# A two-bank maximum on VectorE: one reduction for two heads' score blocks in an attention layer

## What is computed

```python
x = x + attention(layernorm(x)) @ Wo + bo       # causal, scores / sqrt(256), softmax over the keys
x = x + quantised(layernorm(x)) @ quantised(W).T + bias   # blocks of 32, FP6 grid, scale = max|block| / 7.5
```

## Time and profile before

| | |
|---|---|
| median of three runs | 2117.28 us (2115.57 to 2119.65) |
| the profiled execution | 2120.14 us, span 2118.4 us |
| busy: PE, DVE, ACT, POOL | 95%, 82%, 64%, 37% of the span |
| mean granted TensorE clock | 0.985 of full speed |
| whole-unit reductions, L1108 | 1536 of 683 ns, 968.3 us |
| unit products, L1365 | 2560, 816.6 us |

### The profile page before, as it was taken

How to read it: one execution, slowest core, us unless ns; L and a number is a source line. 1 busy time by engine, 2 the same in 40 slices (tenths; PEclk the granted TensorE clock), 3 DMA queues, 4 the chain that set the end, 5 groups by cost and what they waited for, 6 DMA issues and landing times.

```text
span 2118.4 us, 36179 instructions
## 1 busy us (share of the span) xinstructions
PE 2012.2 (95%) x12037; PEld 792.0 (37%) x12037; DVE 1739.8 (82%) x4442; ACT 1365.3 (64%) x2905; POOL 783.3 (37%) x1099
## 2 busy tenths in 40 slices
PE   6799899999999999999999999999999999999994
PEld 3333333333333444343333344434333343333433
DVE  4797897878988787888888788796898998888875
ACT  5357666766766666667665666676666666777661
POOL 3323324231435454543324556363143443111232
PEclk9899999999999999999999999999999999999997
DMA  4441221313040322312122231221403112030000
GB/s 153 128 103 54 59 74 37 94 46 97 19 101 26 97 64 72 101 42 87 49 62 58 79 87 63 66 87 49 118 4 101 42 44 57 25 92 24 9 31 20
DMA packets 178327, 138.72 MB, mean 65 GB/s; under 512 B 54486, under 2 KB 178140, under 8 KB 178140
## 3 DMA queue, kind: packets, MB, share of 16 engines
q1 hardware_dynamic: 178140, 136.40, 23.3%
HBM read 85.20 MB, written 50.33 MB: 64 GB/s over the span
## 4 chain that ended last, share of the span: by engine, by line
PE 72%; DVE 16%; ACT 3%; issue 3%; SPq 2%; POOL 2%; DMA 2%; POOLq 0%; DVEq 0%; ACTq 0%
PE psum L1397 21%; PE psum L1380 19%; PE psum L1365 16%; PE psum L1463 7%; DVE max_parts L1108 7%; PE psum L1456 5%; DVE psum L1103 3%; ACT probs L911 2%; PE psum L1432 1%; SPq L633 1%; PE psum L1415 1%; ACT acc_sb L918 1%; PE psum L1485 1%; DMA out_shop<-ctx_scratch 1%; DVE max_parts L1103 1%
## 5 line engine op out<-in xcount | busy, mean ns | idle before, releaser
L911 ACT ACTIVATE probs<-psum 128x512 f32<-128x512 f32 (+3 forms) x2560 | 1213.3, 537 | 527.4 <-PE psum L1380 521.8
L1108 DVE TENSOR_REDUCE max_parts<-psum 128x1 f32<-128x512 f32 x1536 | 968.3, 683 | 130.0 <-PE psum L1365 125.6
L1380 PE MATMUL psum<-q_rows,k_rows 99*128 99x512 bf16 (+3 forms) x2560 | 857.4, 351 | 3.4 <-ACT probs L911 1.6
L1365 PE MATMUL psum<-k_rows,q_rows 96*128 96x512 bf16 (+3 forms) x2560 | 816.6, 350 | 25.8 <-DVE max_parts L1108 10.2
L1397 PE MATMUL psum<-probs,v_in 128*17 128x512 f32 (+3 forms) x5120 | 595.4, 537 | 10.6 <-ACT acc_sb L918 9.9
L1103 DVE CUSTOM_DVE_ANT_0 psum<-psum,causal 128x128 f32<-128x128 f32 (+3 forms) x1024 | 475.9, 519 | 133.4 <-PE psum L1365 130.2
L1380 PEld LDWEIGHTS psum<-q_rows,k_rows 99*128 99x128 bf16 x2560 | 237.2, 97 | 632.0 <-ACT probs L911 496.3
L748 POOL TENSOR_SCALAR_AFFINE_SELECT probs<-probs 128x512 f32<-128x512 f32 x256 | 165.2, 645 | 788.7 <-ACT probs L911 788.3
L1365 PEld LDWEIGHTS psum<-k_rows,q_rows 96*128 96x128 bf16 x2560 | 245.1, 98 | 277.8 <-DVE max_parts L1108 65.3
L1397 PEld LDWEIGHTS psum<-probs,v_in 128*17 128x17 f32 x5120 | 85.8, 95 | 226.9 <-issue 165.0
L1103 DVE DVE_READ_ACCUMULATOR2_ANT max_parts<- 128x1 f32 x1024 | 145.0, 142 | 0.0
(11 more groups left out here) (158 smaller groups left out, 1374.7 us busy)
## 6 DMA issues: line engine op xcount, KB each, us to landing
q_rows<-qk_scratch SPq DMA_DIRECT2D x384, 64.0 KB, 2.6
k_rows<-qk_scratch SPq DMA_DIRECT2D x384, 64.0 KB, 2.7
qk_scratch<-shop SPq DMA_DIRECT2D x56, 384.0 KB, 2.9
shop<-in_L_attn_x SPq DMA_DIRECT2D x19, 512.0 KB, 4.0
v_scratch<-shop SPq DMA_DIRECT2D x16, 544.0 KB, 4.0
v_in<-v_scratch SPq DMA_DIRECT2D x64, 136.0 KB, 2.6
ctx_scratch<-ctx_out SPq DMA_DIRECT2D x60, 128.0 KB, 1.7
out_shop<-in_L_attn_x SPq DMA_DIRECT2D x12, 512.0 KB, 5.4
```

Source lines behind the costliest of these rows:

```text
L911: nc.scalar.activation(probs[s % NPROBS][:, h, a:CHUNK], bank[SCORE_BANKS[n % 3]][:, a:CHUNK], ACT.Exp, scale=SCALE).then_inc(probs_ready, 1)
L1108: nc.vector.tensor_reduce(max_parts[k % 2][:, first:first + heads, t % TILES, c], ring_bank(UNIT_USE[n])[:, 0:heads * width] .rearrange("p ...
L1365: ins = nc.tensor.matmul(dst[:, i * width:(i + 1) * width], q_rows[u][0:ROWS, qc, first + i, t % TILES * P:(t % TILES + 1) * P], k_rows[u] ...
L1380: nc.tensor.matmul(bank[SCORE_BANKS[n % 3]][:, a:CHUNK], k_rows[u][0:ROWS + LEVELS, h, kb * P:(kb + 1) * P], q_rows[u][0:ROWS + LEVELS, qc ...
```

## The change

Where two neighbouring heads' whole units of one tile and one block of keys stand in the same slot and in neighbouring banks of which the first is 4 or 6 (an even use), VectorE reads both banks with one instruction that has two outputs, and counts `unit_used` up by two. It does so when the second unit's turn comes; the first unit's turn passes without an instruction. All other units are taken as before. PE's program is the same.

```diff
+UNIT_SLOT = {n: p for p in SLOTS for n in UNITS_AT.get(p, [])}
+
+
+def begins_pair(n):
+
+    if n + 1 >= len(UNITS):
+        return False
+    k, t, c, first, heads = UNITS[n]
+    return (c < QCS[k] and UNITS[n + 1] == (k, t, c, first + 1, 1) and UNIT_SLOT[n] == UNIT_SLOT[n + 1]
+            and UNIT_USE[n + 1] == UNIT_USE[n] + 1 and UNIT_USE[n] % 2 == 0)
...
+            def take_pair(n):
+                k, t, c, first, heads = UNITS[n]
+                dve.wait_ge(unit_ready, n + 2)
+                at_bank = RING_BANKS[UNIT_USE[n] % RING]
+                nc.vector.tensor_reduce(max_parts[k % 2][:, first:first + 2, t % TILES, c],
+                                        psum[:, at_bank:at_bank + 2, :], AX.X, ALU.max).then_inc(unit_used, 2)
...
                 for i in range(4):
                     for n in share(units, i, 4):
-                        take_unit(n)
+                        if n > 0 and begins_pair(n - 1):
+                            take_pair(n - 1)
+                        elif not begins_pair(n):
+                            take_unit(n)
```

## The result

The changed kernel takes 2205.45 us (median of four runs, 2204.66 to 2205.95), the kernel before 2116.81 us beside it. The ratio is 1.0405, with a 95% interval of 1.0392 to 1.0419: 86 us slower by the ratio, 89 by the two medians. The forecast was slower by 47 us, 2164; the stated range ended at 2203, and the ratio put on the 2117.28 us of the kernel before is 2203.0, so the result lies at the range's upper end. The sign was right and so was the main place, the size was little over half of what came.

The account below looks back on a forecast made before the run. The prediction took PE, busy 95%, to set the pace mostly, tightly coupled with DVE through four banks. Stalls of 59 us, less 7 hidden and 6 gained, made it 46 to 47 us slower: 2164 us, range 2128 to 2203.

Parts of the forecast that it names:

- The middle pairs' stall: Pairs of heads 1 and 2, values between: bank back after 3.21 us, wanted at 2.83; PE waits 0.38 us every full slot.
- The outer pairs: Pairs of heads 0 and 1 or 2 and 3: 0.70 us to spare in a full slot; 13 short pairs add 4.7 us.
- the 228 pairs before which DVE was behind: Remaining pairs, nothing held back for the second unit: first bank 0.53 us later; taken as zero, upper bound 43 us.
- the rival that gave 2186: DVE's backlog counts: half of the 43 us is added; chance 0.12, shared with two banks costing two instructions.
- The gain of 6 us: DVE's whole-unit reductions on the chain: 87 pairs there save 0.07 us each, 6 us.
- The 7 us taken off: Stalls hidden where values wait for ACT's accumulator copy anyway, or by few other gaps close behind: 7 us less loss.
- DVE's late start: DVE comes 0.52 us later out of a middle pair it waited for; slack covers what stands behind; priced at nothing.
- The shares of the chain: Sign in the profile: PE's share falls, that of DVE's reductions rises from 7% to 15% or more.
- The rival of two whole instructions for a pair: DVE's pair takes 1.37 us, each short pair loses 0.16 more; with backlog 2198; chance 0.12, shared with the backlog rival.
- those of a gain and of absorption: DVE sets the pace and gains: 2111 or 2104, chance 0.08. PE's stalls mostly absorbed: 2115 to 2130, chance 0.08.

Follow-up runs that it names:

- the run with banks given back together: Against the kernel before: every unit reduced singly at its usual turn, but each pair's first unit doesn't count `unit_used` up and its second counts two; 1.0161, 34 us slower.
- the run with few pairs: Against the kernel before: values after head 2 in 206 middle slots, 106 pairs only in slots ending with a long item; 0.9999. Same kernel without pairs: 0.9975.
- the runs with two single reductions: Against the kernel before: each pair waits for its second unit, then is taken as two single reductions; all pairs 1.0095, outer alone 1.0006, middle alone 1.0077.
- the run with middle pairs alone: Against the kernel before: only the 210 pairs of heads 1 and 2 taken with one instruction, all other units single; 1.0289, 61 us slower.

## Why the prediction was right in sign and short in size

**The middle pairs' stall** was right in mechanism and place: 41 + 12 + 1.5 = 54.5 us forecast, less the 7 us of waits that hide a stall some 47, and 61 us measured with these pairs alone. More than half of the difference is one term that was sized too small. DVE's restart after a wait was put at 0.04 us, read at a single unit. A pair starts 0.11 us after its second unit's product, as the units that counted up by two did in the run with banks given back together; so the round is 3.29 us long and not 3.21, and 0.08 us times 111 such pairs is 9 us. The other 5 us were not traced to a term.

**The outer pairs** are the step that failed. The forecast had 4.7 us for them, and for the 228 pairs before which DVE was behind: "the first bank comes back 0.53 us later, which would make PE late by 43 us in all, but DVE still has other units in hand. I take zero". The outer pairs cost 24 us alone, and most of it is this term: with separate releases the loss is gone (1.0006), with a joint release and nothing merged their round is as long as in the change, and of the 28 us by which the rounds of 176 of them grew 22 are in pairs before which DVE was behind. That DVE had work in hand protects DVE. But PE carried 72% of the chain, so a bank that it gets 0.4 us late can be 0.4 us of the end. About half of the 43 us came, as in the rival that gave 2186; zero was as far off as the bound.

**The gain of 6 us** was not found. The pair's length was right to about 1%, but the reductions' time fell by 27 us in all and not 39, and in the run with few pairs they cost 5 us where their cost had been expected to be hidden.

**The 7 us taken off** for waits that hide a stall were about right, 4.9 of them can be seen: in the changed kernel the values wait 5.0 us for the accumulator's copy, 9.9 before.

```profile
L1419 PE MATMUL psum<-probs,v_in 128*17 128x512 f32 (+3 forms) x5120 | 595.3, 537 | 6.3 <-ACT acc_sb L930 5.0
```

**DVE's late start**, the late arrival of what stands behind a pair on DVE, was priced at nothing. It costs 16 us in the middle pairs and nothing in the outer ones, as the runs with two single reductions show. Part of it was in the 54.5 us already, so it isn't to be added in full.

On the signs named ahead: the count, the pair's length and the round of over 3.2 us in slots with middle pairs came as said; PE's waits were to reach some 290 in number and 130 us and reached 404 and 238. DVE was to be less busy by 40 to 80 us and is by 22.7. The shares of the chain can't be compared, since it is followed through only 17%; in the run with middle pairs alone, where it is followed to the start, the reductions have 12% of it and not 15% or more. The rival of two whole instructions for a pair (1.37 us) and those of a gain and of absorption are out. The sentence of the Trainium skill (Perfetto Trace Analysis, Optimizing Scalar/DVE Operations), that breaking instructions up can help where the vector engine isn't saturated but causes bubbles elsewhere, held in this case in its reverse: DVE at 82% merged its work and PE's waits for it tripled.

## What to carry to other kernels

An instruction that empties two buffers of a ring gives back both at its end and can start only when both are full: before merging, add up the first buffer's round (time to the second's filling, the merged instruction, the restarts) and compare it with the time at which its next user wants it. If the engine that fills the buffers sets the pace, count every late release, also where the emptying engine is itself behind: here zero was too low for that term, and the sum of all such delays about twice too high. Where two fills must lie close together, look first at what the filling engine issues between them; moving that one step recovered some 60 us here.

## What the runs showed that was not expected

- Two banks in one reduction cost 1223 ns, which is the 683 ns of one bank and 1.05 ns for each of 512 more columns: crossing from one bank to the next costs nothing that can be seen.
- How long DVE takes to start after a wait depends on what the instruction counts up and not on how long DVE was idle. One that counts the semaphore up by one started 0.04 us after the product that it waited for had ended by the trace; one that counts up by two has its wait as an instruction of its own and started after 0.11 us.
- Issuing the value products after head 2 in every slot, a step that has nothing to do with the maxima, made the kernel 10 us faster than before (0.9952), while no form of the change made it faster.
